# Expert 0 of a routed expert layer in two halves of 256 tokens, with ranks and scatters moved up and the gates' transpose and b2 moved into the later passes

## The reference, cut to what matters

```
logits = flat_x @ W_router + b_router
top_vals, top_idx = jax.lax.top_k(logits, 2)
router_weights = softmax of the two kept logits, 0 elsewhere
for e in range(8):
    h = jax.nn.relu(flat_x @ W1[e] + b1[e])
    y = h @ W2[e] + b2[e]
    final_output = final_output + y * (router_weights[:, e] * chosen)[:, None]
```

## Time and profile before

| | |
|---|---|
| median of 3 runs | 949.31 us (948.82 to 950.19) |
| the profiled execution's own time | 948.45 us |
| span of its trace | 946.6 us (1.85 us of its time lie outside the span) |
| PE busy | 901.7 us, 95% of the span |
| DVE, ACT, POOL busy | 695.9, 519.7 and 603.1 us |
| mean granted TensorE clock | 0.986 of full |

### The profile page before, as it was taken

The page is one execution under the profiler, slowest core; times in us unless marked ns, Lnnn a source line. Parts: engine busy times, 40 slices in busy tenths (PEclk is TensorE's granted clock), DMA queues, the critical chain, the costliest instruction groups (busy, mean ns, idle before and its releaser), DMA issues.

```text
span 946.6 us, 17126 instructions
## 1 busy us (share of the span) xinstructions
PE 901.7 (95%) x6228; PEld 786.8 (83%) x6228; DVE 695.9 (74%) x1211; ACT 519.7 (55%) x915; POOL 603.1 (64%) x647
## 2 busy tenths in 40 slices
PE   6999999999999999999999999999999889899997
PEld 2567888888888888888888888888878669799996
DVE  4658787877978878797786879777577584666765
ACT  2547565565655666565555655666263242366662
POOL 5728778857957876895795789470001066477774
PEclk9999999999999999999999999999999998799999
DMA  5872223312312331232231122110100521365832
GB/s 166 271 251 72 75 79 82 98 40 81 91 53 80 91 83 56 82 85 58 77 84 48 46 60 64 40 37 2 67 1 2 178 90 56 112 222 172 274 124 78
DMA packets 102802, 88.23 MB, mean 93 GB/s; under 512 B 10032, under 2 KB 98112, under 8 KB 102720
## 3 DMA queue, kind: packets, MB, share of 16 engines
q1 hardware_dynamic: 101952, 85.04, 29.9%
q0 software_dynamic: 768, 2.10, 0.7%
HBM read 67.46 MB, written 19.66 MB: 92 GB/s over the span
## 4 chain that ended last, share of the span: by engine, by line
PE 81%; DVE 12%; ACT 2%; issue 2%; POOL 1%; DMA 1%; SPq 0%; POOLq 0%; DVEq 0%; ACTq 0%
PE sps L1512 29%; PE scp L1530 10%; PE scp L1532 9%; PE scp L1531 9%; PE scp L1847 3%; PE sps L1832 3%; PE wps L1832 3%; DVE u_sb L1118 2%; PE wps L1557 2%; PE scp L1848 2%; DVE st L1083 1%; PE sps L1625 1%; PE scp L1480 1%; PE sps L1466 1%; DVE pt_lo L1108 1%
## 5 line engine op out<-in xcount | busy, mean ns | idle before, releaser
L1530 PE MATMUL scp<-cn,pt_hi 128*128 128x258 f32 (+1 forms) x832 | 239.4, 288 | 4.4 <-DVE pt_lo L1108 3.7
L1531 PE MATMUL scp<-cn,pt_hi 128*128 128x256 f32 (+1 forms) x832 | 235.0, 282 | 0.0
L1532 PE MATMUL scp<-cn,pt_lo 128*128 128x258 f32 (+1 forms) x832 | 234.7, 282 | 0.0
L843 ACT ACTIVATE st<-sps 128x512 f32<-128x512 f32 (+1 forms) x208 | 123.4, 593 | 147.4 <-PE sps L1512 146.6
L1108 DVE TENSOR_TENSOR pt_lo<-st,pt_hi 128x512 fp32r<-128x512 f32 (+1 forms) x208 | 194.9, 937 | 6.6 <-ACT pt_hi L852 6.6
L1083 DVE TENSOR_TENSOR st<-st,mbc 128x512 f32<-128x512 f32 (+1 forms) x208 | 157.9, 759 | 39.0 <-ACT mbc L866 38.4
L1512 PE MATMUL sps<-qk_hi,ct_hi 128*128 128x512 f32 (+1 forms) x416 | 168.2, 404 | 11.5 <-DVE cmax L1094 6.6
L849 ACT ACTIVATE st<-st 128x512 f32<-128x512 f32 (+1 forms) x208 | 130.3, 626 | 89.0 <-DVE st L1083 88.4
L1530 PEld LDWEIGHTS scp<-cn,pt_hi 128*128 128x128 f32 (+1 forms) x832 | 156.8, 189 | 14.9 <-DVE pt_lo L1108 6.6
L1512 PE MATMUL sps<-qk_hi,ct_lo 128*128 128x512 f32 (+1 forms) x416 | 164.2, 395 | 0.0
L1512 PE MATMUL sps<-qk_lo,ct_hi 128*128 128x512 f32 (+1 forms) x416 | 163.4, 393 | 0.0
(11 more groups left out here) (301 smaller groups left out, 1485.6 us busy)
## 6 DMA issues: line engine op xcount, KB each, us to landing
w_raw<-W SPq DMA_DIRECT2D x22, 1024.0 KB, 7.5
raw<-ctx_t SPq DMA_DIRECT2D x96, 128.0 KB, 2.2
raw<-ctx_n SPq DMA_DIRECT2D x96, 128.0 KB, 2.1
raw<-qk_scratch SPq DMA_DIRECT2D x56, 128.0 KB, 2.0
xg_scratch<-zrow SPq DMA_DIRECT2D x32, 128.0 KB, 2.3
yg_scratch<-zrow SPq DMA_DIRECT2D x32, 128.0 KB, 2.3
qk_scratch<-stage_b SPq DMA_DIRECT2D x4, 896.0 KB, 4.8
qk_scratch<-stage_a SPq DMA_DIRECT2D x4, 896.0 KB, 4.6
```

The source lines that it names most:

```text
L843: act.activation(st[0:rows(j), par, j, :], sps[0:rows(j), u % 2, :], ACT.Copy).then_inc(out_ok, 1)
L1530: pe.matmul(scp[:, t, 0:D + 2], hi, cn[0:rows(j), j, 0:D + 2], start=j == 0, stop=False)
L1531: pe.matmul(scp[:, t, 0:D], hi, cn[0:rows(j), j, D + 2:CNW], start=False, stop=False)
L1532: ins = pe.matmul(scp[:, t, 0:D + 2], lo, cn[0:rows(j), j, 0:D + 2], start=False, stop=j == SJ - 1)
```

## The change

1. **Two equal halves.** `h_tile` and `y_tile` run for p = 0 (tiles 0 and 1) and p = 1 (tiles 2 and 3), 256 columns each. The special code for tile 3 is gone. The table `LAST` has new places for the steps of tile 3's chain, and `h_tile(0, 3)` waits for the logits of tile 2, since its bank is the one they stand in.
2. **Ranks and scatters moved up.** `first_ranks` comes after n = 1 (was 2), `routes` part a after n = 3 (was 5), and `last_rank` directly after the first half's y (was in the middle of tile 3's h). It writes to `scp[:, 3]`. On POOL scatter(0) comes before tile 3's `chain_rstd`, and the first quarter of unit 1's low weights after scatter(2).
3. **Gates and b2 moved into the passes.** The gates' transpose is in pass 2, the two halves of the b2 product in passes 3 and 4, in the bank that the pass leaves free (`spare(z)`).
4. **First rows transposed within the second half's y.** `transpose_x(0)` stands after f = 4 of `y_tile(1, f)` and writes into `hbank(3)`.
5. **DVE.** `add_y` of tiles 0 and 1 stands after `xt_low(0)`, of tiles 2 and 3 within pass 0's splits (after f = 2 and f = 5). At the end of the kernel `add_gathered` of tiles 0 to 2 is woven around `last_low`, the splits of the last pass's y.

The core of the diff:

```diff
-LAST = dict(zip((2, 4, 6, 7, 8, 11, 12, 14), range(SPREAD - DRAIN, CHAIN_LEN - 1)))
+LAST = dict(zip((1, 2, 4, 5, 6, 11, 13), range(SPREAD - DRAIN, CHAIN_LEN - 1)))
+HALF = MT // 2
...
         def hbank(f):
-            return [trp[0], trp[1], up, wp][f % 4]
+            return [trp[1], up, wp, trp[0]][f % 4]
+        def x_bank(z):
+            return hbank(3) if z == 0 else scp[:, 2 * (z % 2), :]
+        def spare(z):
+            return scp[:, 2 * ((z + 1) % 2) + 1, :]
...
+            scatter(0)
+            chain_rstd(3, 2)
+            for m in range(1, MT - 1):
+                scatter(m)
             low_weights(1, 0)
-            chain_rstd(3, 2)
-            for m in range(MT - 1):
-                scatter(m)
-            low_weights(1, 1)
             scatter(MT - 1)
-            for part in range(2, 4):
+            for part in range(1, 4):
                 low_weights(1, part)
...
             xt_low(0)
+            for m in tiles(0):
+                add_y(m)
             for z in range(NZ):
                 for f in range(FT):
                     split_z(z, f)
+                    if z == 0 and f in (2, 5):
+                        add_y(HALF + f // 3)
                 if z + 1 < NZ:
                     xt_low(z + 1)
+                    if z == GATES_AT:
+                        take_gates()
+                    if z - GATES_AT - 1 in range(2):
+                        if z == GATES_AT + 1:
+                            dve.wait_ge(yc_ok, MT)
+                        add_b2(z - GATES_AT - 1)
...
+            dve.wait_ge(b2_added, 2)
+            for m in range(HALF):
+                add_gathered(m)
+            last_low(0)
+            add_gathered(HALF)
+            last_low(1)
             for m in range(MT):
+                if m == MT - 1:
+                    add_gathered(m)
                 dve.wait_ge(comb_ok, m + 1)
...
             def transpose_x(z):
 
                 pe.wait_ge(xg_in[z % 2], 16 * (z // 2 + 1))
-                if z < 2:
-                    pe.wait_ge(yc_ok, 2 * (z + 1))
+                if z == 0:
+                    pe.wait_ge(hl_ok, 2 * FT)
+                elif z == 1:
+                    pe.wait_ge(yc_ok, HALF + 1)
...
-            transpose_x(0)
+            for f in range(FT):
+                y_tile(1, f)
+                if f == FT // 2:
+                    transpose_x(0)
             for z in range(NZ):
                 for f in range(FT):
-                    if z == 0 and f == 2:
-                        pe.wait_ge(b2_added, 2)
                     h_z(z, f)
                 if z + 1 < NZ:
                     transpose_x(z + 1)
+                    if z == GATES_AT:
+                        transpose_gates(z)
+                    if z - GATES_AT - 1 in range(2):
+                        times_b2(z, z - GATES_AT - 1)
```

More of the change, by code:

```diff
@@ L1412, in make_place, with add_gathered @@
                 for a in range(2):
-                    dve.tensor_scalar(place[:, a, :], scp[:, 2 * ((z + 1) % 2) + 1, :], rows_col[:, a:a + 1], None,
+                    dve.tensor_scalar(place[:, a, :], spare(z), rows_col[:, a:a + 1], None,
                                       ALU.is_equal).then_inc(place_ok, 1)
-            xt_low(0)
-            for z in range(NZ):
-                for f in range(FT):
-                    split_z(z, f)
-                if z + 1 < NZ:
-                    xt_low(z + 1)
-                    if z == PLACE_AT:
-                        make_place(z)
-                    finish_y(z)
-                if z == PLACE_AT - 1:
-                    spread_places()
-            dve.wait_ge(yc_ok, MT)
-            b0 = 2 * ((NZ - 1) % 2)
-            for a in range(2):
-                dve.wait_ge(y_hi_ok, a + 1)
-                dve.tensor_tensor(y_lo[:, a, :], scp[:, b0 + a, 0:D], y_hi[:, a, :].bitcast(F32),
-                                  ALU.subtract).then_inc(y_lo_ok, 1)
-            for m in range(MT):
+            def add_gathered(m):
                 dve.wait_ge(gathered[m], 32)
@@ L1439, in _, with last_low @@
                                              in1=x_sb[:, m, :], op0=ALU.mult, op1=ALU.add).then_inc(add_ok, 1)
+            b0 = 2 * ((NZ - 1) % 2)
+            def last_low(a):
+                dve.wait_ge(y_hi_ok, a + 1)
+                dve.tensor_tensor(y_lo[:, a, :], scp[:, b0 + a, 0:D], y_hi[:, a, :].bitcast(F32),
+                                  ALU.subtract).then_inc(y_lo_ok, 1)
+            xt_low(0)
+            for m in tiles(0):
+                add_y(m)
+            for z in range(NZ):
+                for f in range(FT):
+                    split_z(z, f)
+                    if z == 0 and f in (2, 5):
+                        add_y(HALF + f // 3)
+                if z + 1 < NZ:
+                    xt_low(z + 1)
+                    if z == GATES_AT:
[4 more added lines that the diff above has]
+                        add_b2(z - GATES_AT - 1)
+                    if z == PLACE_AT:
+                        make_place(z)
+                    finish_y(z)
+                if z == PLACE_AT - 1:
+                    spread_places()
+            dve.wait_ge(b2_added, 2)
[4 more added lines that the diff above has]
+            last_low(1)
             for m in range(MT):
+                if m == MT - 1:
+                    add_gathered(m)
                 dve.wait_ge(comb_ok, m + 1)
@@ L1800, in _, with transpose_gates, times_b2 @@
-            ins.then_inc(gates_pe, 1)
+                h_tile(1, f)
+            def transpose_gates(z):
+                pe.wait_ge(chain_dve[MT - 1], DVE_NO["gw"])
+                pe.wait_ge(yb_ok, z)
+                for m in range(MT):
+                    ins = pe.transpose(spare(z)[0:NE, m * P:(m + 1) * P], gw[:, m, :], ident[:])
+                ins.then_inc(gates_pe, 1)
+            def times_b2(z, x):
+                pe.wait_ge(gwT_ok, 1)
+                pe.wait_ge(yb_ok, z)
+                for m in (2 * x, 2 * x + 1):
+                    ins = pe.matmul(spare(z)[:, m % 2 * D:(m % 2 + 1) * D], gwT[:, m * P:(m + 1) * P], b2_sb[:],
+                                    start=True, stop=True)
+                ins.then_inc(gates_pe, 1)
@@ L1820, in transpose_places @@
                 for m in range(MT):
-                    ins = pe.transpose(scp[:, 2 * ((z + 1) % 2) + 1, m * P:(m + 1) * P], at_row[:, m, :], ident[:])
+                    ins = pe.transpose(spare(z)[:, m * P:(m + 1) * P], at_row[:, m, :], ident[:])
                 ins.then_inc(at_pe, 1)
```

167 lines of the change are left out of this document (58 added, 109 removed).

## The result

The changed kernel takes **945.49 us** (median of 20 runs, 940.57 to 948.31), the kernel before 949.48 beside it (20 runs, 946.35 to 951.72). The ratio is 0.9955 with a 95% interval of 0.9941 to 0.9969: 4.0 us faster by the medians and 4.3 by the ratio, where 11.5 were forecast. 945.49 lies above the range of 934.4 to 942.5, between the forecast and the rival of the long low clock (943 to 945.5).

The account below looks back on a forecast made before the run. PE was taken to bound the kernel (81% of the chain of waits). Gains of 13.0 + 1.9 - 2.1 + 0.3 = 13.1 us from 948.45 give 935.3 at full clock; 2.4 for the clock makes 937.8, range 934.4 to 942.5.

Parts of the forecast that it names:

- the rival of the long low clock: Clock falls in expert 0 and stays low for long: 943 us, up to 945.5; chance 0.13.
- First half: Expert 0, tiles 0 and 1: PE starts h at 768.21, OT at 776.4 after waiting 1.5 us for `cbd`, y at 781.2.
- `cnt` ended 8.2 us after Y's stretch before: Tile 3's `cnt` ready at 788.0, so PE waits half a microsecond and ends the last rank at 789.8.
- Second half: Expert 0, tiles 2 and 3: h follows DVE's splits, first rows don't delay PE, pass 0 starts at 802.0, 13.0 us gained.
- Pass 0, 12.4: Pass 0 takes 12.4 us instead of 14.25, with 0.5 us for `add_y` delaying the splits: 1.9 us gained.
- Gates and b2, -2.1: Gates' transpose 0.44 us in pass 2 and b2's products 1.7 us in passes 3 and 4: 2.1 us lost, bounds 2.0 and 3.0.
- Tail, +0.3: At the end, the new order of `add_gathered` gains 0.3 us, bounds -0.5 and 1.2.
- The clock, -2.4: Two short falls of the granted clock in expert 0, at the narrow places, cost 2.4 us together.
- First fall: Low clock among C0, ranks, OT and waits, 769.6 to 777.5: short kind, 3.4 us, half covered by PE's wait, costing 0.9.
- Second fall: Low clock at the wait and last rank near 787.5: short kind, 3.4 us, costing 1.5.
- The rival that the clock never falls: Clock stays high in the changed kernel: 935.3 us, with small terms 934.2 to 936; chance 0.22.

Follow-up runs that it names:

- The profile at high clock: Profiled run of the changed kernel, run again unchanged: 939.83 us, the fastest of its runs, whose median was 945.06 us.
- chip D: Chip of the last group: kernel before again 0.9997, changed kernel 0.9959, with GpSimd's first unit 1 block ahead of the first scatter 0.9941, fastest version 0.9866.
- the unread products: Changed kernel plus ten fp32 products of 256 columns that nobody reads, in three PE waits ahead of expert 0: ratio 0.9925 to the kernel before, 943.00 us.
- moving the block: Changed kernel with GpSimd's first block of unit 1's low weights ahead of the first scatter: ratio 0.9929 to the kernel before, on another chip 0.9941.
- shortening the rank: Changed kernel with GpSimd's block ahead of the first scatter and six of the last rank's eight products ahead of the wait for `cnt`: ratio 0.9900, 940.17 us.
- The control: The changed kernel run again unchanged on another chip: ratio 0.9956 to the kernel before, 945.06 us (939.83 to 949.77).
- group C: Kernels on one chip: changed plus one satisfied wait 0.9951; plus unread products 0.9925; these, block and short rank 0.9897; also b2 behind the last y 0.9875.
- groups A and D: Experiments on two chips, both with the changed kernel and its variant with GpSimd's block ahead of the first scatter: changed 0.9956 and 0.9959, variant 0.9929 and 0.9941.

## Why the prediction was wrong

It was right in the sign and in the order of the work, wrong in the clock and in one wait, and 7.7 us too low. The profile at high clock separates the two parts of the error: 939.83 against the 935.3 forecast at full clock is 4.5 us of mis-sized terms; from there to 945.49 it is 5.7 us, where I had 2.4 for the clock. (The two numbers come from different chips, whose medians of the changed kernel are 945.49 and 945.06.)

- **First half: right.** h at 768.1, OT 776.3, Y 778.2 to 779.8, y 781.4, at full clock within 0.2 us of each forecast.
- **"`cnt` ended 8.2 us after Y's stretch before": failed.** At full clock it ended 10.0 us after (779.79 to 789.81), of which 1.6 go with the low weights moved beside it (8.4 to 6.8 us after y's start when they are moved back). The wait is 1.97 us instead of 0.5, and the last rank ends at 791.67 instead of 789.8: **1.9 of the 4.5**. I had looked at what POOL's new order delays, not at what it runs beside. The sentence that the low weights of unit 1 "now follow the last scatter" also passes over the first quarter, which stands ahead of it, and it is this quarter that runs beside `cnt`.
- **Second half: right.** DVE-paced, from the last rank's end to pass 0 12.63 us; forecast 12.2. Forecast start 802.0, at high clock 804.30, the **0.4** here and the 1.9 above. PE waits neither for the first rows nor for their splits.
- **Pass 0, 12.4:** 12.88. The pace of DVE costs PE 0.7 us in it (wait for h_lo) instead of 0.5, and 0.3 more elsewhere. **0.5.**
- **Gates and b2, -2.1:** -3.0, of which 0.44 is the transposes, as forecast, and 2.5 b2, its upper bound. Y's products were the wrong neighbour: 0.40 us each, where two of b2 take 1.05 (861.23 to 862.28) and 0.2 goes around them; why was not tried. **0.9.**
- **Tail, +0.3:** -0.6 by these two profiles (21.43 against 20.86), -0.75 on chip D, +0.7 where ScalarE was prompt. **0.9**, which hangs on the chip.
- **The clock, -2.4: failed, and it is the largest part.** I had two short falls, one at each narrow place, 0.9 and 1.5 us. The runs showed 5.7 between the high-clock profile and the median. Twelve profiles are of the changed kernel or a variant without the unread products.
  - *First fall: wrong in place and size.* It is missing in three of the twelve, 3.4 us long in two, 10.2 in two, 13.7 in three and 17.1 in two. It begins at 766.9 to 767.1 in four, ahead of the first h block, and 1.0 us behind the start of h in three (768.3, 769.2, 770.2), when only 256-column blocks of h have run. Only in the two short ones, at 773.1 and 773.4, does it begin among the narrow products, where I had put it.
  - *Second fall: right in place, too short.* It begins at the last rank or up to 3.3 us behind its start in eight of the twelve, and is 3.4 us long in four, 6.8 in four.
  - *What stands ahead of the first fall* are PE's waits in the chains, of 0.76, 0.86 and 0.97 us between 763 and 769. With these filled, none of four profiles has the first stretch, and their 18 runs have mean clocks of 0.991 to 0.996. Only one of the four kernels differs in nothing else, but moving the block and shortening the rank did not take the stretch away by themselves (it stands in the three profiles without the unread products). The products also move all behind them by 1.1 us; that this and not the filling took the stretch away was not tried.
  - *The waits are not enough for a fall.* The kernel before has them too, and its first stretch begins at 796.9 in one profile and at 769.4, 1.0 us behind the start of h, in the other. The control has them and no stretch in expert 0 at all. What decides in one execution stays open.
- **The rival of the long low clock**, chance 0.13, has the measured time in its 943 to 945.5, partly by luck: it adds 7.5 to 10.2 us of clock to 935.3, where the runs have 4.5 of other terms and 5.7 of clock.
- **The rival that the clock never falls** is the case in single runs (three of 20 at 0.995 or more, five of 29 with the control), but at 939.8 to 942.1 us, not at 934.2 to 936. By the rule of the Trainium skill, "TensorE: Matmul & The Clock Gate", Part 1, idling brings the clock down. The unread products agree with it in direction for the first stretch: PE busy for 1.78 of 3.40 us ahead of a fall, for 3.40 of 3.40 where none came (the rows in group C). But the control had 1.53 of 3.40 and no fall, and the fall at 796.9 in before came with PE busy throughout. Which of the two narrow places costs more was not tried apart.

Open: what delays ScalarE in the tail, and why one chip has none of it; how much of the moved block's gain is the wait and how much the clock, since groups A and D gave 2.5 and 1.2 us.

## What to carry over

Moving a block on one engine changes what the others run beside, not only what it delays: look up both prices of each small step on the path. Where the granted clock differs between runs of one kernel, forecast the stretches' lengths from several executions and look for their cause ahead of the changed code; filling waits with unread products was worth 2.3 us here, beside 4 for the change. Compare tails only between profiles of one chip.

## What the runs showed of the hardware

- Small DVE steps beside GpSimd arithmetic: two `onehot` and `cnt` on 8 columns take 1.33 and 0.64 us beside subtractions of 256 columns on GpSimd, 0.36 and 0.17 without. `cnt` took 0.17 beside an indirect DMA's issue too (before, 791.14).
- The same program on the same chip ran at mean clocks of 0.984 to 0.997, and took 949.8 to 939.8 us.
- ScalarE's second y_hi, which waits for TensorE's last y product alone, started 0.04 us behind it on one chip, 2.6 us on another and 4.1 us on two more, the same for every program of a group.
- An fp32 product of 256 columns that starts an accumulation took 0.43 us (three unread ones in 1.29), one of b2 with 8 rows 0.53 (two in 1.05).
